# A recommendation model's forward pass: interactions cut into slices between the gathers of the next tile

## The reference

```python
h = relu(dense @ dw1 + db1)
dense_emb = relu(h @ dw2 + db2)                    # 64 numbers
sparse_emb = emb_tables[f_ids, sparse_idx]         # 26 rows of 64, one of 12500 in each table
emb = concatenate([dense_emb[:, None, :], sparse_emb], axis=1)   # 27 x 64
inter = einsum('bfd,bgd->bfg', emb, emb)
pairs = inter[:, iu0, iu1]                         # 351 pairs
z = concatenate([emb.reshape(B, -1), pairs], axis=1)
z = relu(z @ ow1 + ob1); z = relu(z @ ow2 + ob2); z = relu(z @ ow3 + ob3)
return z @ ow4 + ob4                               # 512, 256, 128, 1 wide
```

## Time and profile before

| | |
|---|---|
| median of three runs | 192.86 us |
| the profiled execution's own time | 192.67 us |
| its span, first to last instruction | 190.9 us |
| PE busy | 128.6 us (67%) |
| POOL busy | 128.1 us (67%), 104 gathers and as many scratch writes |
| ACT, DVE busy | 49.6 us, 43.9 us |
| mean granted TensorE clock | 0.874 of 2.4 GHz |

### The profile page before, as it was taken

The page is one execution under the profiler, slowest core; times in us unless marked ns, Lnnn a source line. Parts: engine busy times, 40 slices in busy tenths (PEclk is TensorE's granted clock), DMA queues, the critical chain, the costliest instruction groups (busy, mean ns, idle before and its releaser), DMA issues.

```text
span 190.9 us, 3083 instructions
## 1 busy us (share of the span) xinstructions
PE 128.6 (67%) x1301; PEld 69.3 (36%) x1301; DVE 43.9 (23%) x97; ACT 49.6 (26%) x96; POOL 128.1 (67%) x213
## 2 busy tenths in 40 slices
PE   1500295957348993854639985968389899669994
PEld 0000132424135432442534432324355356245343
DVE  2700004001064105001236014001541051245211
ACT  0440400040078101030286010030781110365211
POOL 3888888888565888888467888887658887000000
PEclk9999999699855799999555996669969999988999
DMA  5999432312311322222222423213123322000000
GB/s 169 411 330 355 124 26 23 25 22 25 22 14 16 25 26 21 26 28 21 17 21 21 24 25 25 25 21 25 16 17 25 27 23 23 6 3 3 0 0 0
DMA packets 4576, 9.80 MB, mean 51 GB/s; under 512 B 2065, under 2 KB 2065, under 8 KB 3922
## 3 DMA queue, kind: packets, MB, share of 16 engines
q0 software_dynamic: 3328, 3.41, 21.0%
q1 hardware_dynamic: 1010, 5.30, 6.9%
q10 hardware_dynamic: 224, 0.89, 1.5%
HBM read 9.59 MB, written 0.00 MB: 50 GB/s over the span
## 4 chain that ended last, share of the span: by engine, by line
PE 48%; POOL 21%; issue 18%; ACT 8%; DVE 2%; DMA 1%; ACTq 0%
PE acc L258 22%; POOL gathered L211 16%; PE acc L290 10%; PE inter L274 7%; POOL pace L215 5%; PE acc L308 4%; ACT emb L382 2%; ACT emb L381 2%; DVE pairs L183 2%; DMA dense_sb<-dense_pack 1%; PE inter L226 1%; PE inter L223 1%; PE turned L239 1%; ACT z L394 1%; ACT L371 1%
## 5 line engine op out<-in xcount | busy, mean ns | idle before, releaser
L211 POOL DMA_INDIRECT gathered<-tables,rows x104 | 99.3, 955 | 33.0 <-issue 16.0
L258 PE MATMUL acc<-w,emb 128*128 128x512 f32 x104 | 65.8, 784 | 19.4 <-ACT emb L382 9.3
L258 PEld LDWEIGHTS acc<-w,emb 128*128 128x128 f32 x104 | 31.4, 315 | 45.3 <-issue 30.1
L387 ACT ACTIVATE pairs<-inter 28x96 f32<-28x96 f32 (+1 forms) x64 | 23.2, 362 | 38.8 <-PE inter L274 38.2
L183 DVE COPY pairs<-inter 28x96 f32<-28x96 f32 (+1 forms) x64 | 23.1, 361 | 31.5 <-PE inter L274 30.8
L215 POOL MEMSET pace<- 128x192 uint8 x104 | 28.6, 275 | 0.1
L274 PE MATMUL inter<-emb 64*28 64x28 f32 x1024 | 13.3, 212 | 19.4 <-POOL pace L215 13.2
L290 PE MATMUL acc<-w,pairs 128*128 128x512 f32 x56 | 24.8, 593 | 0.3 <-DVE pairs L183 0.3
L274 PEld LDWEIGHTS inter<-emb 64*28 64x28 f32 x1024 | 12.0, 125 | 24.6 <-POOL pace L215 11.4
L381 ACT ACTIVATE emb<-turned 128x512 f32<-128x512 f32 x8 | 8.8, 1095 | 45.8 <-PE turned L239 25.7
L460 DVE COPY emb<-turned 128x512 f32<-128x512 f32 (+1 forms) x7 | 5.5, 785 | 60.3 <-issue 36.6
(11 more groups left out here) (47 smaller groups left out, 26.3 us busy)
## 6 DMA issues: line engine op xcount, KB each, us to landing
w<-w SPq DMA_DIRECT2D x5, 1024.0 KB, 10.7
gathered<-tables,rows POOLq DMA_INDIRECT x104, 3.4
small<-small_pack ACTq DMA_DIRECT2D x1, 706.5 KB, 7.0
dense_sb<-dense_pack ACTq DMA_DIRECT2D x1, 160.5 KB
idx_raw<-idx SPq DMA_DIRECT2D x1, 39.0 KB
idx_raw<-idx SPq DMA_DIRECT2D x1, 13.0 KB, 1.8
out<-y SPq DMA_DIRECT2D x1, 2.0 KB
```

Source lines behind the costliest of these rows:

```text
L211: pool.indirect_dma_start(out=gathered[:, t, s, :], out_offset=None, in_=tables, in_offset=bass.IndirectOffsetOnAxis(ap=rows[:, t, s:s + 1 ...
L258: nc.tensor.matmul(acc[t][:], emb[:, tile_of(t), place(2 * c)], w[:, c, :], start=(c == 0), stop=False)
L387: last = move(lambda dst, src: nc.scalar.activation(dst, src, ACT.Copy), t, k, (0, 1))
```

## The change

Its parts, with what they do:

- In tiles 1 and 2 POOL no longer waits. The interactions of tiles 0 and 1 are done by PE in 16 slices of 8 samples; slice i waits until gather s=4+i of the next tile has raised `gathers_held`, which the gather does itself (`engine_sem`, raised by the issuing engine, beside the semaphore that counts the landing).
- In tile 3 the two holds stay (s=7 and 10), raised by the gather; behind these two gathers no scratch write stands.
- The scratch write has 256 bytes; there is none from s=18 of tile 3 on.
- A bank holds other samples: quadrant j has samples 32j + 16k to 32j + 16k + 15, so that `move` writes runs of 16 samples. The number of copies and their elements stay.
- PE's order in tiles 1 and 2: slices 0 to 5, turn 0, slices 6 and 7, four times one slice and one chunk's products, slices 12 and 13, turn 1, slices 14 and 15, products of group 1, pair products, turn 2, z1's transposes, products of group 2, turn and products of group 3. In tile 3 products of group 1 are placed between layer 2, layer 3, layer 4 and the turns.
- ACT keeps group 0 before its first moves and DVE keeps group 1 between its two halves of moves, in tiles 1 and 2.

```diff
+GROUP = P // 4
+HALF = GROUP // 2
-PACE = 192
+PACE = 256
+SLICES = 16
+SLICE_FROM = 4
+UNPACED_FROM = 18
...
             for j in quads:
+                first = j * GROUP + k * HALF
                 for q in range(4):
                     top = QUAD_SLOTS[q]
-                    src = bank[QUAD * j:QUAD * j + PLACES, 0:(b1 - b0) // 4 * PLACES] \
-                        .rearrange("p (n g) -> p n g", g=PLACES)[:, :, SLOTS * q:SLOTS * q + top]
-                    dst = pairs[QUAD * q:QUAD * q + PLACES, t, 0:top, b0:b1] \
-                        .rearrange("p s (n j) -> p n s j", j=4)[:, :, :, j]
-                    last = copy(dst, src)
+                    src = inter[k][QUAD * j:QUAD * j + PLACES, 0:HALF * PLACES] \
+                        .rearrange("p (n g) -> p g n", g=PLACES)[:, SLOTS * q:SLOTS * q + top, :]
+                    last = copy(pairs[QUAD * q:QUAD * q + PLACES, t, 0:top, first:first + HALF], src)
...
+                        held = t == LAST and s in HOLDS
+                        released = 0 < t < LAST and SLICE_FROM <= s < SLICE_FROM + SLICES
                         pool.indirect_dma_start(
...
+                            engine_sem=gathers_held if held or released else None,
                         ).then_inc(group_in[t][g], 16)
-                        paced = nc.gpsimd.memset(pace[:, t * NF + s, :], 0)
-                        if t and s in HOLDS:
-                            paced.then_inc(gathers_held, 1)
+                        if held:
                             pool.wait_ge(inter_done, 2 * (t - 1) + HOLDS.index(s) + 1)
+                        elif t < LAST or s < UNPACED_FROM:
+                            nc.gpsimd.memset(pace[:, t * NF + s, :], 0)
...
+            def grams(t, k, n0, n1):
+                for n in range(n0, n1):
+                    for j in range(4):
+                        b = t * P + j * GROUP + k * HALF + n
+                        mm = nc.tensor.matmul(inter[k][QUAD * j:QUAD * j + PLACES, n * PLACES:(n + 1) * PLACES],
+                                              emb[0:D, b, :], emb[0:D, b, :], start=True, stop=True)
+                if n1 == HALF:
+                    mm.then_inc(inter_done, 1)
...
+            def slices(t, first, end):
+                if first == 0:
+                    ready(t)
+                for i in range(first, end):
+                    pe.wait_ge(gathers_held, SLICES * t + i + 1)
+                    k, n = divmod(2 * i, HALF)
+                    grams(t, k, n, n + 2)
...
+            for t in range(1, LAST):
+                slices(t - 1, 0, 6)
+                turn(t, 0)
+                slices(t - 1, 6, 8)
+                for c in range(*GROUPS[0]):
+                    slices(t - 1, 8 + c, 9 + c)
+                    field_products(t, 0, (c, c + 1))
+                slices(t - 1, 12, 14)
+                turn(t, 1)
+                slices(t - 1, 14, SLICES)
+                field_products(t, 1)
+                pair_product(t - 1)
+                turn(t, 2)
+                z1_to_features(t - 1, at_once)
+                field_products(t, 2)
+                turn(t, 3)
+                field_products(t, 3)
...
             layer2(early, LAST - 1, [[(m, k) for m in range(2) for k in range(K1)]], (acc[0], acc[1]))
-            field_products(LAST, 1)
+            c0, c1 = GROUPS[1]
+            field_products(LAST, 1, (c0, c0 + 1))
             layer3(early, 0, acc[2])
+            field_products(LAST, 1, (c0 + 1, c0 + 3))
+            turn(LAST, 2)
             layer4(early, 0, acc[0])
-            turn(LAST, 2)
+            field_products(LAST, 1, (c0 + 3, c1))
             turn(LAST, 3)
```

More of the change, by code:

```diff
@@ L35 @@
 W_GROUPS = CHUNKS // W_GROUP
-BANK_FROM = [0, P // 2, P]
+GROUP = P // 4
+HALF = GROUP // 2
 EARLY = LAST * P
-PACE = 192
+PACE = 256
+SLICES = 16
+SLICE_FROM = 4
 HOLDS = [7, 10]
+UNPACED_FROM = 18
 Z1_STEPS = [(0, 1), (1, 2), (2, 4)]
@@ L172, in move @@
         def move(copy, t, k, quads):
-            b0, b1 = BANK_FROM[k:k + 2]
-            bank = inter[k]
             for j in quads:
+                first = j * GROUP + k * HALF
                 for q in range(4):
                     top = QUAD_SLOTS[q]
-                    src = bank[QUAD * j:QUAD * j + PLACES, 0:(b1 - b0) // 4 * PLACES] \
-                        .rearrange("p (n g) -> p n g", g=PLACES)[:, :, SLOTS * q:SLOTS * q + top]
-                    dst = pairs[QUAD * q:QUAD * q + PLACES, t, 0:top, b0:b1] \
-                        .rearrange("p s (n j) -> p n s j", j=4)[:, :, :, j]
-                    last = copy(dst, src)
+                    src = inter[k][QUAD * j:QUAD * j + PLACES, 0:HALF * PLACES] \
+                        .rearrange("p (n g) -> p g n", g=PLACES)[:, SLOTS * q:SLOTS * q + top, :]
+                    last = copy(pairs[QUAD * q:QUAD * q + PLACES, t, 0:top, first:first + HALF], src)
             return last
@@ L259, in field_products, with ready @@
                                      start=(c == 0), stop=False)
+            def ready(t):
+                if t == 0:
+                    pe.wait_ge(dense_placed, 1)
+                kept(t, 2)
+                kept(t, 3)
+                if t:
+                    moved(t - 1)
+            def grams(t, k, n0, n1):
[6 more added lines that the diff above has]
+                    mm.then_inc(inter_done, 1)
             def interactions(t, k):
                 if k == 0:
[L264 to L269, removed]
-                if t < LAST:
[L271 to L276, removed]
+                    ready(t)
+                if t < LAST:
+                    pe.wait_ge(gathers_held, SLICES * t + k + 1)
+                grams(t, k, 0, HALF)
+            def slices(t, first, end):
+                if first == 0:
+                    ready(t)
+                for i in range(first, end):
+                    pe.wait_ge(gathers_held, SLICES * t + i + 1)
+                    k, n = divmod(2 * i, HALF)
+                    grams(t, k, n, n + 2)
             def moved(t):
@@ L327, in _ @@
             at_once = [(0, K1)]
-            for t in range(TILES):
-                if t:
-                    interactions(t - 1, 0)
-                turn(t, 0)
[L334 to L339, removed]
-                turn(t, 1)
[L341 to L346, removed]
+            for g in range(NG):
+                turn(0, g)
+                field_products(0, g)
+            for t in range(1, LAST):
+                slices(t - 1, 0, 6)
+                turn(t, 0)
+                slices(t - 1, 6, 8)
[3 more added lines that the diff above has]
+                slices(t - 1, 12, 14)
+                turn(t, 1)
+                slices(t - 1, 14, SLICES)
[6 more added lines that the diff above has]
+                field_products(t, 3)
+            interactions(LAST - 1, 0)
+            turn(LAST, 0)
+            interactions(LAST - 1, 1)
+            field_products(LAST, 0)
+            pair_product(LAST - 1)
+            z1_to_features(LAST - 1, at_once)
+            turn(LAST, 1)
             layer2(early, LAST - 1, [[(m, k) for m in range(2) for k in range(K1)]], (acc[0], acc[1]))
-            field_products(LAST, 1)
+            c0, c1 = GROUPS[1]
+            field_products(LAST, 1, (c0, c0 + 1))
             layer3(early, 0, acc[2])
+            field_products(LAST, 1, (c0 + 1, c0 + 3))
+            turn(LAST, 2)
             layer4(early, 0, acc[0])
-            turn(LAST, 2)
+            field_products(LAST, 1, (c0 + 3, c1))
             turn(LAST, 3)
@@ L414, in _ @@
             for t in range(TILES):
-                if t:
+                if t == LAST:
                     moves(t - 1, 0)
                 keep(t, 0)
+                if 0 < t < LAST:
+                    moves(t - 1, 0)
                 if t:
@@ L491, in _ @@
                     moves(t - 1, 0)
+                if 0 < t < LAST:
+                    keep(t, 1)
+                if t:
                     moves(t - 1, 1)
                     z1_features(t - 1, at_once)
-                keep(t, 1)
+                if t in (0, LAST):
+                    keep(t, 1)
                 if t == LAST:
```

## The result

The changed kernel takes 237.4 us (median of four runs, 235.4 to 240.7) against 192.6 (192.0 to 193.0) of before. Two of the four runs were in the chip's slower state, and over the fast runs alone the change takes 1.224 times as long, with an interval of 1.217 to 1.230. The profiled execution has a span of 233.6 us. I had forecast 185.6, in a range of 182.0 to 190.5.

What follows compares the result with a forecast made beforehand. PE and POOL take turns, meeting at the holds; PE bounds the last tile. Last interactions at 161.45, tail 22.46, moves -0.2 give a span of 183.7; with 1.77 around it 185.5, stated as 185.6 us, range 182.0 to 190.5.

Steps and rivals of the forecast that it cites:

- part 2: Tiles 1 and 2, slices: 0.2 us each, little but waiting; slice 15 free at 107.55, PE through with tile 2 at 129.0.
- rival D: Interactions beside gathers: releases come only with the landing, 190.3 us, chance 0.04; grown gathers, near 198, counted with C.
- Part 1: POOL without holds in tiles 1 and 2: 9.4 us gone, step 1.45 with the longer write, s=7 of tile 3 at 126.9.
- Part 3: Last tile: held interactions at 129.0 and 134.6, new order saves waits, last interactions at 161.45 against 168.44, gain 7.0 us.
- The unpaced step: Tile 3, POOL's last gathers without scratch writes: 1.12 us each if the gap stays; dropping eight writes worth nothing by itself.
- its cover: Tile 3: last gather lands at 157.9, PE turns group 3 at about 160.3, so 2.4 us of slack.
- Part 4: Moves in runs of 16 samples: 8 take 2.1 to 3.0 us; gain 0 to 0.3 at the end, 0.2 taken.
- C: PE's clock stays low through tiles 1 and 2 because of short work and waits: 200 us; chance 0.14 together with slowed gathers.

## Why the prediction was wrong

**The step that failed is in part 2:** "A slice is 16 of the 128 matmuls that take 1.71 at the slow clock: 0.2 us." On average a slice took 4.6 (72.8 over 16). The row was read rightly, but it came from a hold, and the change took the holds away. All such rows did. I noted in rival D that no row had interactions beside gathers and then priced only POOL's side of it, longer gathers; the gathers stayed at 0.95 and PE paid. There was a hint in the trace of before that I left unused, in the first bursts of tiles 0 and 1, each started 0.4 us after a gather's end:

```profile
50.95 1.03 PE L274 MATMUL inter<-emb 64*28 64x28 f32 x42 [2.82 <-issue]
52.41 1.26 PE L274 MATMUL inter<-emb 64*28 64x28 f32 x86 [0.44 <-issue]
...
92.02 0.69 PE L274 MATMUL inter<-emb 64*28 64x28 f32 x40 [2.89 <-POOL pace L215]
93.09 1.27 PE L274 MATMUL inter<-emb 64*28 64x28 f32 x88 [0.39 <-issue]
```

42 and 40 matmuls, a pause of some 0.4 us that nothing explains, and the rest at full pace: PE runs dry near the same number as in the changed kernel, but POOL stood still and the supply came back. It is a hint and no more. In the run with tile 3's order alone the same bursts start as long after a gather's end and go through whole (50.63, 128 in 1.26 us). And 14.5 us of holds, which order no data, are a question: what does POOL's standing protect? I put them down as a price and never asked what they bought.

**Part 1 held.** The step was 1.44 (forecast 1.45, the write 0.328 us); s=7 of tile 3 started at 125.98 (126.9).

**The rest of part 2 held where the state is not entered.** With slices from 7 on, slice 15 starts at 111.37 and the held interactions at 131.36: 20.0 us from the slice's start, where I had summed 21.0 from its end. The change with four writes fewer takes 182.1 us where the kernel before takes 189.2, 7.1 less; I had forecast 7.2 less than the profiled execution. So near a match is partly luck: the run with one write fewer takes 5.7 less and the one with slices from 5 on 6.3. But the parts describe the kernel that the change would be with its first burst half a microsecond to the side.

**Part 3 held in kind.** The order brought 2.3 us up to the last interactions, as summed, and 3.0 in the whole. I had kept the tail behind them at 22.46; in the changed kernel it takes 20.6 (213.02 to 233.6), 1.5 of it in the four product matmuls that ran at the full clock. The unpaced step is 1.25 and not 1.12, which its cover hid.

**Part 4.** The moves came out at the fast end. PE's products beside the last ones (2.96) end no earlier, so all that can be gained is the wait behind them: 0.33 before, none in the changed kernel. The medians with and without them, 186.2 and 186.3, can't tell the 0.2 I took from nothing.

```profile
L184 DVE COPY pairs<-inter 28x112 f32<-28x112 f32 x32 | 8.8, 276 | 0.4
...
L184 DVE COPY pairs<-inter 28x96 f32<-28x96 f32 x32 | 8.2, 255 | 52.1 <-remote 39.4 <-PE inter L278 12.4
```

276 and 255 ns against 380 and 341. The reads from the bank, strided by 28 places, show no cost beside what the contiguous copies would give (0.27 and 0.25). The Trainium skill's line rule (SBUF — State Buffer, Door 1: The DMA port swizzle) holds here for the writes and not for these reads; the measurement decides.

**Rivals.** C named the sign and the wrong cause. The clock was low (0.52 from 51 to 126), but in the run with slices from 7 on it was not up either (0.69 between 52.5 and 74.2), and the 14 pair products took 6.17 in both. The other clause of its chance, gathers growing, did not happen. The 0.14 for slower was too little for a resource that no row showed: PE's supply of small instructions beside gathers had a lower bound (nothing lost) and no upper bound at all, and I gave it a few in a hundred.

**Open:** by what path a gather keeps instructions from PE, and why a burst that begins up to 0.02 us after a gather's start falls in and one at 0.25 does not. One path the traces nearly rule out. Instructions arrive in transfers of 16 KiB on a queue of their own (q8), and bursts do pause for them where no gather runs. In the run without holds:

```profile
190.45 1.12 PE L273 MATMUL inter<-emb 64*28 64x28 f32 x110
193.40 0.32 PE L273 MATMUL inter<-emb 64*28 64x28 f32 x18 [1.83 <-issue]
```

Such a transfer ran from 190.67 to 192.05, and PE came back 1.35 us later; a second one (227.52 to 228.69) has a pause of 1.52 us, over 1.32 us behind its end. These pauses are single. In the dribble of the changed kernel q8 moved one block from 52.39 to 53.36, in 0.97 us, and nothing more until 88.8. The lists of DMA queues for 52.3 to 53.4 and for 53.4 to 88.8 have (packets, MB, share):

```profile
q8 instruction: 1, 0.02, 5.5%
...
q0 software_dynamic: 782, 0.80, 27.0%
```

q8 is in the first and not in the second, and PE got 1 to 5 interaction matmuls at a time all through it. So blocks that come late are not what makes the dribble; the way from a block to PE is not in these traces. I didn't try other small instructions on PE than these products and the transposes that dribbled along, nor whether ACT's or DVE's are held back.

## What to carry to other kernels

Where a kernel pays for a wait that orders no data, measure what it protects before you remove it: take it out alone, in one run (here 284.8 us), before anything is built on its absence. A duration read in a stretch where another engine stood still is no duration beside that engine; look for a row with both, and if none exists, the price has no upper bound from the trace. Bursts of small matmuls belong where POOL issues no gather; or should be fewer and wider.

## What the runs showed of the hardware that I had not expected

- Beside POOL's indirect gathers PE ran through 40 to 43 matmuls of 28 columns in 0.55 us and then got 1 to 7 at a time, some 5 per step of 1.44 us with 256-byte writes, and at most 4 per step of 1.39 with 192-byte ones. Products of 512 columns beside the same gathers showed nothing (14 in 6.17 us).
- The state keeps itself: the same slices are served in 0.3 to 0.4 us when it is not entered. A burst that began 0.02 us after a gather's start made 237 us, one at 0.48 made 184.
- Plain transfers from SP of the same size, and scratch writes of POOL, cause none of it.
- Bursts of small matmuls also run dry where no gather is issued: twice in the run without holds, for 1.83 and 1.52 us, until 1.3 to 1.4 us after a 16 KiB transfer of the instruction queue had ended.
- Gathers with no write between them follow at 1.25 us, with a gap of 0.30 instead of 0.17.
